# Attention scores of two heads from two 64-row tiles, keys split without doubling, weighted sum issued one step later

## The reference, cut to what matters

```python
q = x1 @ Wq                                  # x1 = layernorm(x): 128 x 256; q: 128 x 1024
kv = x2 @ Wkv                                # x2 = ctx_1024: 12544 x 256
k, v = jnp.split(kv, 2, axis=-1)
q, k, v = map(_split_heads, (q, k, v))       # 16 heads of 64
attn = jnp.einsum('bhid,bhjd->bhij', q, k) * SCALE
attn = jax.nn.softmax(attn, axis=-1)
out = jnp.einsum('bhij,bhjd->bhid', attn, v)
out = out.transpose(0, 2, 1, 3).reshape(b, l, h * d)
return out @ Wo + bo
```

## Time and profile before

| | |
|---|---|
| median of 3 runs | 1564.63 us (1563.09 to 1567.99) |
| the profiled execution's own time | 1565.5 us |
| its span (first to last instruction) | 1563.8 us |
| PE busy | 1468.7 us (94%) |
| DVE busy | 1242.0 us (79%) |
| ACT busy | 970.9 us (62%) |
| POOL busy | 604.6 us (39%) |
| mean granted clock of PE | 0.971 of full speed |

### The profile page before, as it was taken

One profiled execution on the slowest core, in us unless ns is written; L12 is line 12 of the kernel. 1 busy time (PEld: TensorE's weight loads), 2 busy tenths in 40 slices (PEclk: granted clock), 3 DMA queues, 4 the chain that ended last, 5 costly groups with the idle time before them and its releaser, 6 DMA issues. The chain is left out here.

```text
span 1563.8 us, 24194 instructions
## 1 busy us (share of the span) xinstructions
PE 1468.7 (94%) x8657; PEld 1303.5 (83%) x8657; DVE 1242.0 (79%) x2278; ACT 970.9 (62%) x1807; POOL 604.6 (39%) x519
## 2 busy tenths in 40 slices
PE   6999999999999999999999999999977989999479
PEld 5988998899889888988898889889865878888248
DVE  6888888888888888888888888888975356666764
ACT  4777777777777777777777777777651245555121
POOL 6334343434343434343434343433300256665330
PEclk9999999999999999999999999999997899999779
DMA  5000000000000000000000000000007122220600
GB/s 182 1 1 25 1 25 1 24 1 24 1 25 1 25 1 25 1 25 1 25 1 25 1 25 1 1 1 1 1 28 296 74 72 70 70 70 24 282 1 4
DMA packets 9099, 57.13 MB, mean 37 GB/s; under 512 B 2120, under 2 KB 2719, under 8 KB 7968
## 3 DMA queue, kind: packets, MB, share of 16 engines
q1 hardware_dynamic: 8992, 55.73, 9.6%
HBM read 55.60 MB, written 0.13 MB: 36 GB/s over the span
## 5 line engine op out<-in xcount | busy, mean ns | idle before, releaser
L314 POOL CAST V<-Vraw 128x512 fp32r<-128x512 f32 x189 | 115.8, 613 | 654.4 <-ACT Vraw L405 654.4
L369 ACT CAST K<-ps 64x448 fp32r<-64x448 f32 x448 | 236.4, 528 | 142.6 <-PE ps L532 133.1
L397 ACT ACTIVATE pT<-ps 128x896 fp32r<-128x896 f32 x224 | 206.3, 921 | 161.9 <-PE ps L558 161.7
L435 DVE TENSOR_TENSOR K<-ps,K 64x448 fp32r<-64x448 f32 x448 | 278.8, 622 | 13.3 <-ACT K L369 3.4
L493 DVE TENSOR_TENSOR pT<-ps,pT 128x896 fp32r<-128x896 f32 x224 | 244.6, 1092 | 31.9 <-ACT pT L397 8.3
L315 POOL TENSOR_TENSOR V<-Vraw,V 128x512 fp32r<-128x512 f32 x189 | 242.2, 1281 | 15.2
L443 DVE TENSOR_REDUCE nmx<-ps 128x1 f32<-128x896 f32 x224 | 242.2, 1081 | 0.0
L643 PEld LDWEIGHTS ps<-pT,V 128*128 128x128 f32 x1568 | 214.3, 189 | 17.0 <-DVE pT L493 7.5
L643 PE MATMUL ps<-pT,V 128*128 128x256 f32 x1568 | 222.5, 281 | 6.1 <-DVE pT L493 6.1
L379 ACT ACTIVATE prob<-ps,nm 128x896 f32<-128x896 f32 x224 | 224.3, 1001 | 0.0
L602 PE MATMUL ps<-ident,prob 128*128 128x128 f32 x1568 | 209.0, 274 | 0.0
(11 more groups left out here) (306 smaller groups left out, 2389.9 us busy)
## 6 DMA issues: line engine op xcount, KB each, us to landing
raw<-in_ctxT SPq DMA_DIRECT2D x14, 896.0 KB, 4.7
d_raw<-in_ctxT SPq DMA_DIRECT2D x14, 896.0 KB, 4.6
w<-in_w SPq DMA_DIRECT2D x2, 4096.0 KB, 16.8
wg<-in_wg SPq DMA_DIRECT2D x1, 4352.0 KB, 25.7
wu<-in_wu SPq DMA_DIRECT2D x1, 4352.0 KB, 16.8
wd<-in_wd SPq DMA_DIRECT2D x1, 4352.0 KB, 26.7
e_ea<-in_alog SPq DMA_DIRECT2D x1, 2048.0 KB, 7.3
wq<-in_wq SPq DMA_DIRECT2D x1, 1024.0 KB, 5.2
```

Of the source, the lines that this page charges most:

```text
L369: nc.scalar.copy(K[halves[s], slot, cols], ps[halves[s], piece_bank(p), 0:HK]).then_inc(sem("kh_ready"), 1)
L397: nc.scalar.activation(pT[:, :, 0, :], pT_ps, ACT.Copy).then_inc(sem("pTh_ready"), 1)
L435: ins = nc.vector.tensor_tensor(K[halves[1 - s], slot, cols], ps[halves[s], piece_bank(p), 0:HK], K[halves[s], slot, cols].bitcast(F32), A ...
```

## The change

Queries and keys are kept as the matmuls deliver them: a key piece has head 2m in partitions 0 to 63 and head 2m+1 in partitions 64 to 127, and the high parts lie in `Kh`, the low parts in `Kl`. One operation of 128 partitions makes each. `scores(pair)` makes the scores of both heads of a pair: for each half of the keys it issues three products (qh Kh, qh Kl, ql Kh), each as two matmuls of 64 rows by 448 columns, one in array rows 0 to 63, one in rows 64 to 127, into different PSUM banks. It is issued in every second step. `pT` has two buffers, and the weighted sum of step `u - 1` is issued in step `u`, behind the scores and ahead of the key piece; the values follow at the end of the step. The transposes now wait for the low part of the step before and for the update of `U` of step `u - 3`. The step of eight without values is the one with `u % 8 == 6`. `AHEAD` is 4. The block that declares the later stages' tiles now stands behind the call of the first stage; its code is the same.

```diff
-    AHEAD = 5
+    AHEAD = 4
-    v_steps = [u for u in range(steps - HG) if u % HG < NT]
+    V_AT = (0, 1, 2, 3, 4, 5, 7)
+    v_steps = [u for u in range(steps - HG) if u % HG in V_AT]
...
-        K = sb("K", [P, 2 * RING, CK], F32R, keep)
+        Kh = sb("Kh", [P, RING, CK], F32R, keep)
+        Kl = sb("Kl", [P, RING, CK], F32R, keep)
-        pT = sb("pT", [P, NT, 2, P], F32R, keep)
+        pT = [sb(f"pT{i}", [P, NT, 2, P], F32R, keep) for i in range(2)]
...
-                for s in range(2):
-                    for d in range(2):
-                        nc.scalar.activation(by_pair(qh)[halves[d], :, s, :], q_ps(ps)[halves[s]], ACT.Copy,
-                                             scale=SCALE).then_inc(sem("qh_ready"), 1)
+                nc.scalar.activation(qh[:, :, :], q_ps(ps), ACT.Copy, scale=SCALE).then_inc(sem("qh_ready"), 1)
                 def high_parts(p):
...
-                    for s in range(2):
-                        slot, cols = piece_of(p, s)
-                        nc.scalar.copy(K[halves[s], slot, cols], ps[halves[s], piece_bank(p), 0:HK]).then_inc(
-                            sem("kh_ready"), 1)
+                    slot, cols = piece_of(p)
+                    nc.scalar.copy(Kh[:, slot, cols], ps[:, piece_bank(p), 0:HK]).then_inc(sem("kh_ready"), 1)
...
-                    dve.wait_ge(sem("kh_ready"), 2 * p + 2)
-                    for s in range(2):
-                        slot, cols = piece_of(p, s)
-                        ins = nc.vector.tensor_tensor(K[halves[1 - s], slot, cols], ps[halves[s], piece_bank(p), 0:HK],
-                                                      K[halves[s], slot, cols].bitcast(F32), ALU.subtract)
+                    slot, cols = piece_of(p)
+                    nc.vector.tensor_tensor(Kl[:, slot, cols], ps[:, piece_bank(p), 0:HK], Kh[:, slot, cols].bitcast(F32),
+                                            ALU.subtract).then_inc(sem("kl_ready"), 1)
...
-                def scores(u):
+                def scores(pair):
+                    m, slot = pair % PAIRS, pair % RING
                     for half in range(2):
-                        keys = K[:, key_slot(u), half * HK:(half + 1) * HK]
-                        nc.tensor.matmul(S[b][:, half, :], qh[:, h, :], keys, start=True, stop=False)
-                        mm = nc.tensor.matmul(S[b][:, half, :], ql[:, h, :], keys, start=False, stop=True)
+                        keys, n = slice(half * HK, (half + 1) * HK), 0
+                        for w, x in ((qh, Kh), (qh, Kl), (ql, Kh)):
+                            for s in range(2):
+                                mm = nc.tensor.matmul(S[s][:, half, :], w[halves[s], m, :], x[halves[s], slot, keys],
+                                                      start=(n == 0), stop=(n == 2))
+                            n += 1
                     mm.then_inc(sem("scores_done"), 1)
...
                 for u in range(steps):
...
                     pe.wait_ge(sem("exp_done"), u + 1)
-                    if u >= 2:
-                        pe.wait_ge(sem("u_added"), u - 1)
+                    if u >= 1:
+                        pe.wait_ge(sem("pTl_ready"), u)
+                    if u >= 3:
+                        pe.wait_ge(sem("u_added"), u - 2)
...
+                    if u >= 2:
+                        mm = turn_sums(u - 2)
+                    mm.then_inc(sem("p_turned"), 1)
+                    if u % 2 == 1 and u + 1 < steps:
+                        pe.wait_ge(sem("kl_ready"), u + 3)
+                        scores((u + 1) // 2)
                     if u >= 1:
+                        weighted_sum(u - 1)
...
+                pe.wait_ge(sem("u_added"), steps - 2)
+                turn_sums(steps - 2).then_inc(sem("p_turned"), 1)
+                weighted_sum(steps - 1)
```

More of the change, by code:

```diff
@@ L136, in build @@
         stage_context(nc, t, sb, sem, link, ps, norms, v)
+        keep("wg0", [P, KT, E0])
+        keep("bg", [P, E0])
+        keep("b2", [E0, D])
+        keep("wx", [P, KT, D])
+        keep("bx", [P, KT])
+        keep("wxp", [P, KT, DTR + 2 * NST])
+        keep("wdt", [DTR, D])
+        keep("bdt", [1, D])
+        keep("dskip", [P, D])
+        keep("wr1", [P, KT, E1])
+        keep("br1", [P, E1])
         with ExitStack() as experts:
@@ L395, in _ @@
                 for u in range(steps):
[L396 to L401, removed]
+                    if u - 1 in v_steps:
+                        j = v_steps.index(u - 1)
                         act.wait_ge(sem("v_done"), NT + j + 1)
@@ L405, in _ @@
                         nc.scalar.copy(Vraw[:, j % 2, :], ps[:, 6, :]).then_inc(sem("vraw_ready"), 1)
+                    act.wait_ge(sem("p_turned"), u + 1)
+                    nc.scalar.activation(pT[u % 2][:, :, 0, :], pT_ps, ACT.Copy).then_inc(sem("pTh_ready"), 1)
+                    if u + 1 < steps:
+                        exp_step(u + 1)
                     if u + AHEAD < steps:
@@ L470, in _ @@
                 split_key_weight(left, 1)
[L471 to L475, removed]
+                dve.wait_ge(sem("qh_ready"), 1)
+                nc.vector.scalar_tensor_tensor(ql[:, :, :], q_ps(ps), SCALE, qh[:, :, :].bitcast(F32), ALU.mult,
+                                               ALU.subtract).then_inc(sem("ql_ready"), 1)
                 split_key_weight(right, 2)
@@ L500, in _ @@
                                             rs[:, b:b + 1], ALU.mult, ALU.add)
-                    if u + 2 < steps:
-                        max_step(u + 2)
-                    m = (u - (steps - H0)) // 2 - 1
-                    if u > steps - H0 and u % 2 == 0:
-                        scale_sums(m)
+                    if u + AHEAD < steps:
+                        low_parts(u + AHEAD)
+                    if u >= steps - H0 + 3 and u % 2 == 1:
+                        scale_sums((u - (steps - H0) - 3) // 2)
+                update_sums(steps - 2)
                 add_parts(steps - 1)
@@ L558, in turn_sums, with weighted_sum @@
                     return nc.tensor.transpose(O_ps, osb[:, :], ident[:, :])
+                def weighted_sum(u):
+                    h, g = u % H0, u // HG
+                    pe.wait_ge(sem("pTl_ready"), u + 1)
+                    if u in v_steps:
+                        pe.wait_ge(sem("vraw_ready"), v_steps.index(u) + 1)
+                    if h % HG == 0:
+                        if g == 0:
+                            pe.wait_ge(sem("first_vl"), NT)
+                        else:
+                            pe.wait_ge(sem("v_split"), NT * g)
+                    for k in range(NT):
+                        mm = nc.tensor.matmul(OT_ps, V[g % 2][:, k, h % HG, :],
+                                              pT[u % 2][:, k, :, :].rearrange("p a q -> p (a q)"),
+                                              start=(k == 0), stop=(k == NT - 1))
+                    mm.then_inc(sem("pv_done"), 1)
                 def turn_heads(pairs, bank):
@@ L577, in _ @@
                 piece(3)
[L578 to L579 removed]
+                pe.wait_ge(sem("ql_ready"), 1)
+                pe.wait_ge(sem("kl_ready"), 2)
+                scores(0)
                 pe.wait_ge(sem("wv_split"), 1)
                 for i in range(NT):
[L582 to L586 removed]
                     if i < 3:
@@ L627, in _ @@
                         piece(p)
+                    if u in v_steps:
+                        j = v_steps.index(u)
+                        gn, i = g + 1, V_AT.index(u % HG)
+                        if j == 0:
+                            pe.wait_ge(sem("first_vl"), NT)
+                        else:
+                            pe.wait_ge(sem("vraw_ready"), j)
+                        if u >= 1:
+                            pe.wait_ge(sem("o_added"), u)
+                        if gn % 2 == 0 and i == 0:
+                            pe.wait_ge(sem("cT_split"), gn + 2)
+                        values(gn, i, 6)
                     if u == steps - 1:
```

93 lines of the change are left out of this document (17 added, 76 removed).

## The result

| | before | changed |
|---|---|---|
| median | 1565.05 us (9 runs, 1561.96 to 1567.99) | 1570.52 us (9 runs, 1568.42 to 1572.93) |
| ratio to before | | 1.0044, 95% interval 1.0027 to 1.0060 |
| profiled execution, span | 1563.8 | 1568.2 |

The changed kernel is 0.4% slower, 5.5 us; 1560 was forecast, 5 us faster. The time lies in the range, but the change went the other way.

What follows compares the result with a forecast made beforehand. PE's stream was taken as the bound in seven steps of eight. Scores -1, waits 0, start -5, end +1.5 make -4.5 against the profiled 1565.5 us: 1561, or 1560 as median; range 1522 to 1588.

Steps and rivals of the forecast that it cites:

- One slot per term: Scores of a pair: each product's two 64-row matmuls run side by side in one 0.205 us slot, six slots, not twelve.
- The price of changing the tile's height: Around a pair's scores: 0.20 us going in, 0.27 for emptying; pair 1.83 against 1.84, -1 us in all.
- Waits ... Net 0: Steady steps: PE's transposes newly wait for DVE's update of `U`, 22 us, just what the two old waits cost.
- What DVE and ACT do beside it costs nothing: First stage, seven steps of eight: PE's stream is the bound, with no time left for a wait in the 5.12 us.
- The step without values: Step `u % 8 == 6`: PE has 2.93 us against DVE's chain of 3.76 and waits 0.8, 28 times; step about 3.7.
- Odd steps: Steps with scores: 1.71 us from `osb` to the weighted sum, DVE's chain covered by 0.2, about 5.9 in all.
- Start and end: Before step 0 less DVE and ACT work, -5 us (-3 to -7); at the end one weighted sum and transpose alone, +1.5.
- loads in single file: Rival: weight loads on disjoint rows can't run together, 0.218 us per term; +19 us, 1580 in all; chance 0.18.
- no overlap: Rival: the scores' matmuls run one after the other, twelve slots per pair; +138 us, about 1700; chance 0.13.
- a cheap change: Rival: the 64-row tile doesn't wait for the array to empty; pair 1.47 us, -41 us, 1520 in all; chance 0.23.
- The fourth rival: A wait in every odd step if DVE's operations exceed their 0.2 us cover; 11 us per 0.1, 1571 for 0.3; chance 0.08.
- slower (0.34): Chance given to the whole change being slower than the kernel before, against 0.43 for faster and 0.23 for same.

Runs made afterwards that it cites:

- the shorter copy: Changed kernel with ACT's copy of the values out of PSUM bank 6 taking 256 of 512 columns (output differs): 1558.61 us, ratio to before 0.9949.
- the late wait: Changed kernel with the wait for the update of `U` moved from before the seven transposes to before the fifth: 1561.22 us, ratio to before 0.9970.

## Why the prediction was wrong

- **One slot per term**: right. 0.20 per term after the first; with both on the same rows it is 0.41. The Trainium skill's statement ("TensorE: Matmul & The Clock Gate", part 3, the mechanism) that matmuls in different row groups start about 4 ns apart agrees with the trace, whose single records start 3 ns apart.
- **The price of changing the tile's height**: right in size. Forecast for the odd step from `osb` to the weighted sum, with the next weights' load, was 1.71, measured is 1.62 and 0.11 more in the first slot, 1.73. Taken away as a whole it gives 33 us. The rule that changing the tiling mode drains the engine (the Trainium skill, "TensorEngine Tiling (Array Packing)", key properties) fits: the loader stands idle 0.17 and 0.31 at the two changes, and the runs give them a price, 0.39 us on PE there and back, 0.29 in the kernel's time.
- **"Waits ... Net 0"**: this is the step that failed, a wait that the sum put at nothing. The text followed DVE's chain and found it covered; it did not follow ACT's. "What DVE and ACT do beside it costs nothing" was true for the old order only. The weighted sum moved away from behind the key piece, which covered the copy of the values out of bank 6, to a place 0.88 us behind the values, while hand-over (0.19), copy (0.59) and the way back (0.12) take 0.90, and the loader would have started some 0.1 before the 0.88 were over: it did at 608.97, 0.90 behind the first transpose, where with the shorter copy it is 0.77. New was a wait for this copy: 0.11 in even steps, 0.13 in the step without values, 84 x 0.11 + 28 x 0.13 = 13 us, against 11.9 measured by the shorter copy and 13.3 in its trace. Without the wait the 216 steps take 1091.8 us, 2.1 less than before, where the other terms of the forecast have 1 less, and the forecast's 1560 compares with 1558.6. A part of how close that comes is luck, since start and end have errors of their own.
- **The step without values**: the wait for `U` is there as forecast (0.66 and, on the loader, up to 1.0), once per eight steps; 0.25 us of it was not needed, as the late wait shows.
- **Odd steps**: 5.94 for 5.91. The sum was made from the rows of one step of 5.12; the six undisturbed steps with values in each eight of the kernel before last 5.12 to 5.14 between steps 40 and 200, 5.13 in the mean. A pair takes 10.27 there and not 10.24, so about 0.03 per pair is in both kernels and not in the difference.
- **Start and end**: -5.6 for -5 in the traced execution, with 2.9 as the lower end of the gain. The end was put at +1.5 and came out at -2.3, and the clock accounts for that, no gain of the change does. The windows view gives the granted clock of that end (columns as in rows 2): 0.72 before, where the 18 us hold stretches at the lower of the two levels (1.2 GHz), and 0.89 in the changed kernel. From the last transposes on (1169 and 1175) it is 0.72 and 1.00.

The stage's end before:

```profile
1163.00:1181.00 18.00, 15.02 (x62) 11.73 (x61) 7.04 (x19) 4.23 (x8) 0.00 (x0) 0.72 0.00 1
```

and in the changed kernel:

```profile
1169.00:1184.00 15.00, 11.76 (x61) 9.55 (x61) 8.59 (x25) 4.55 (x10) 0.00 (x0) 0.89 0.00 0
```

The same eight matmuls of the output projection at either clock:

```profile
1172.33 3.78 PE L568 MATMUL ps<-wo,oT 128*128 128x256 f32 x8
```

```profile
1177.46 1.99 PE L563 MATMUL ps<-wo,oT 128*128 128x256 f32 x8
```

From start to start these eight take 3.22 before and 1.83 in the changed kernel, the last seven transposes 1.36 and 0.79, the weighted sum 1.42 and 0.91: 2.5 us for three groups of the same matmuls. Without them the end would be 0.2 longer than before, and not 2.3 shorter. In all traces of the changed kernel and its variants that were read here the end takes 8.3; whether the kernel before always meets the lower clock there one trace can't say.

- **Rivals**: loads in single file, no overlap and a cheap change fell in the first timeline of the changed kernel. The fourth rival had the right form, a wait in half of the steps with 11 us per 0.1, but on the wrong engine and in the wrong steps.
- **The range** held; the chances did not favour slower (0.34), because the wait that decided was listed nowhere.

## What to carry to other kernels

When an instruction is moved on the engine that bounds the kernel, list for every buffer it touches, PSUM banks included, who must have left it, and what stood between before and now. Here the cover was lost on ACT, which is busy for only 551 of 900 us, and a wait of 0.1 us in a hundred steps was more than the change was to gain. Half-height tiles on disjoint rows do share a slot, but each change of height costs PE 0.4 us here, so they pay only where the slots saved per change are worth more. To put a wait in front of the first instruction that needs it, instead of in front of the group, was worth 9 us here.

## What the runs showed of the hardware that was not expected

The order of the half-height matmuls in the queue makes no difference: three on one half of the rows followed by three on the other take the same time as alternating ones (1569.6 in one run against 1570.5 us, terms every 0.20), and the first matmul on the other half starts 10 ns behind the first on this half, ahead of two that were issued before it. Their weight loads start together too, 0.19 us for two, 0.18 for one. A wait for a bank can hide in the waits view: the engine that waits was busy with the instruction before until almost the end, and the 0.11 us per step, 12 us in all, stood under no name.
